# Attention softmax denominators out of the weighing product, and a new order of TensorE's blocks in a one-core audio tower

## What is computed

```
h = silu([x, 1] W_h + b_h) W_o + b_o + [x, 1] W_r + b_r        # patches of 16 samples, hidden 512
a = layernorm(h); q, k, v = a per head times Wq, Wk, Wv         # 16 heads of 16, 64 tokens per batch row
h = h + softmax(q k / sqrt(256)) v W_out + b_out
h = h + real(ifft(fft(layernorm(h)) w)) + bias
```

## Time and profile before

| | |
|---|---|
| median of 3 runs | 142.65 us (142.65 to 142.79) |
| the profiled execution: its own time | 142.76 us |
| the profiled execution: its span | 141.0 us |
| mean granted clock of TensorE | 0.993 of full |
| busy, share of the span | PE 94%, PEld 80%, DVE 79%, POOL 67%, ACT 61% |
| DMA packets | 24508 |

### The profile page before, as it was taken

The page is one execution under the profiler, slowest core; times in us unless marked ns, Lnnn a source line. Parts: engine busy times, 40 slices in busy tenths (PEclk is TensorE's granted clock), DMA queues, the critical chain, the costliest instruction groups (busy, mean ns, idle before and its releaser), DMA issues.

```text
span 141.0 us, 6132 instructions
## 1 busy us (share of the span) xinstructions
PE 132.8 (94%) x2444; PEld 112.4 (80%) x2444; DVE 111.6 (79%) x337; ACT 85.7 (61%) x245; POOL 94.7 (67%) x186
## 2 busy tenths in 40 slices
PE   6879999999999998999999999999999999999861
PEld 2469999999997876978878889889788788788540
DVE  5584596859978578798898898988988988978751
ACT  4374765477878584865947747649558477455110
POOL 3284796996583364677687686786876876773361
PEclk9999999999999999999999999999999999999997
DMA  4678000030000010121312302203113123031102
GB/s 70 157 174 257 14 0 0 0 36 11 2 0 5 5 19 5 19 50 15 63 37 23 60 12 49 56 7 65 46 15 60 37 23 59 6 60 41 38 0 74
DMA packets 24508, 5.89 MB, mean 42 GB/s; under 512 B 20384, under 2 KB 24224, under 8 KB 24480
## 3 DMA queue, kind: packets, MB, share of 16 engines
q1 hardware_dynamic: 24192, 5.37, 18.3%
q10 hardware_dynamic: 288, 0.13, 0.3%
HBM read 2.35 MB, written 2.10 MB: 32 GB/s over the span
## 4 chain that ended last, share of the span: by engine, by line
PE 78%; DVE 7%; POOL 4%; issue 3%; DMA 3%; ACT 1%; SPq 1%; POOLq 0%; DVEq 0%
PE bank L1036 11%; PE bank L954 11%; PE bank L1022 7%; PE bank L1099 6%; PE bank L1075 5%; PE bank L959 5%; PE bank L1080 4%; PE bank L1120 4%; PE bank L1064 3%; DMA wf_raw<-in_W_r 3%; PE bank L1049 2%; PE bank L1133 2%; PE bank L948 2%; PE bank L1103 2%; PE bank L1124 2%
## 5 line engine op out<-in xcount | busy, mean ns | idle before, releaser
L824 DVE TENSOR_REDUCE bank<-bank 128x4 f32<-128x256 f32 x64 | 22.8, 425 | 6.9 <-ACT pT L376 6.5
L376 ACT ACTIVATE pT<-bank 128x256 f32<-128x256 f32 x64 | 19.4, 391 | 2.5 <-PE bank L1049 2.5
L1036 PE MATMUL bank<-qT,xzT 32*128 32x64 f32 x512 | 17.9, 276 | 0.0
L1036 PEld LDWEIGHTS bank<-qT,xzT 32*128 32x128 f32 x512 | 15.7, 186 | 2.7 <-issue 2.7
L695 DVE TENSOR_TENSOR hid_lo<-bank,hid_hi 128x512 fp32r<-128x512 f32 x16 | 11.0, 685 | 7.5 <-ACT bank L344 7.5
L582 POOL TENSOR_TENSOR side_lo<-sideT,side_hi 128x256 fp32r<-128x256 f32 x14 | 10.2, 728 | 8.3 <-ACT sideT L386 8.3
L545 POOL TENSOR_SCALAR xblk<-xh,parity_sb 128x128 f32<-128x128 f32 x32 | 11.5, 372 | 5.9 <-PE bank L1080 4.8
L371 ACT ACTIVATE maxT<-bank 128x128 fp32r<-128x128 f32 x16 | 4.4, 277 | 17.8 <-PE bank L1058 17.8
L593 POOL TENSOR_TENSOR on_lo<-onT,on_hi 128x256 fp32r<-128x256 f32 x14 | 10.3, 737 | 7.1 <-ACT on_hi L390 6.8
L553 POOL TENSOR_TENSOR hb_all<-h_all,bout_bc 128x256 f32<-128x256 f32 x16 | 11.5, 735 | 4.0 <-ACT h_all L348 4.0
L361 ACT ACTIVATE xzT<-bank,parity_sb 128x256 f32<-128x256 f32 x28 | 12.0, 498 | 0.0
(11 more groups left out here) (166 smaller groups left out, 386.8 us busy)
## 6 DMA issues: line engine op xcount, KB each, us to landing
out<-y SPq DMA_DIRECT2D x16, 128.0 KB, 1.7
xblk<-xh SPq DMA_DIRECT2D x32, 32.0 KB, 2.5
wo_raw<-in_W_o SPq DMA_DIRECT2D x1, 512.0 KB, 4.2
wout_raw<-in_W_out SPq DMA_DIRECT2D x1, 256.0 KB, 2.9
fr<-in_wr SPq DMA_DIRECT2D x1, 256.0 KB, 4.3
fi<-in_wi SPq DMA_DIRECT2D x1, 256.0 KB, 4.3
minus_raw<-in_minus_rows SPq DMA_DIRECT2D x1, 128.0 KB, 2.2
bout_bc<-in_b_out SPq DMA_DIRECT2D x1, 128.0 KB, 3.5
```

Source lines behind the costliest of these rows:

```text
L376: nc.scalar.activation(pT[:, j, :], bank[j][:, D:2 * D], ACT.Exp).then_inc(exp_done, 1)
L824: nc.vector.tensor_reduce(rowmax[:, j, :], bank[j][:, 0:D].rearrange("p (h k) -> p h k", k=TOK), AX_X, ALU.max).then_inc(max_done, 1)
L1036: pe.matmul(bank[j][:, at0:at0 + TOK], xzT[t % 3][rows32, 2 * half + b, :, :].rearrange("p e k -> p (e k)"), qT[t % 3][rows32, half, TOK * ...
```

## The change

The denominators come out of the same products that weigh x. xblk is now, for each of two batch rows and 16 heads, 32 columns wide: 16 of x and 16 of ones, which a memset sets once. A product covers the 64 rows of one head's keys instead of the 128 of two, so there are 32 of them; the even heads' results go to one PSUM bank, the odd heads' to another, and in both 16 rows are weighed x and 16 the denominator. VectorE transposes both banks at once (128x512) and takes reciprocals of one column per block; GpSimd multiplies (VectorE in the last two tiles); VectorE transposes the quotients into onT. Nothing crosses heads any more, so there are no zeros to keep, and all placing is done by four DMAs per tile. TensorE's project moves to the front of the following step, mix_freq takes tile i-2 instead of i-1, turn_side behind query. The queues of the other engines follow. xh, h2b and rstd2 have three buffers, the row maxima move into the score banks, and x, the sides and the maxima change banks.

```
+    on_rows, weighedT, xh[3], h2b[3], rstd2[3];  xblk: [P, 2, D] -> [P, 2, 2*QUADS, 2*HD], memset to 1.0
-    pair_ones (constant, load and tile), sumsT, inv_rows
@@ sync
-            def place_crossed(t):      # two DMAs
+            def place(t):
                 sp.wait_ge(xh_set, t + 1)
                 if t >= 2:
                     sp.wait_ge(pv_done, t - 1)
+                heads = xh[t % 3][:].rearrange("p (g e d) -> p g e d", e=2, d=HD)
                 for b in range(2):
+                    for e in range(2):
+                        sp.dma_start(xblk[t % 2][TOK * e:TOK * e + TOK, b, :, 0:HD],
+                                     heads[TOK * b:TOK * b + TOK, :, e, :]).then_inc(xblk_placed[t % 2], 16)
+            for i in range(T + 3):
                 if i + 2 < T:
-                    place_crossed(i + 2)
-                if i >= 1:
-                    store(i - 1)
+                    place(i + 2)
+                if i >= 3:
+                    store(i - 3)
@@ scalar, step(i) after:
+    copy_xT(i+3), copy_max(i+1), copy_xzT(i+3), exponent(i+1), lead_on(i), copy_q(i+3), copy_side(i-1)
+    copy_q(t) waits for side_turned t-3 (from t = 4)
@@ gpsimd
-            def place_same(t): ...
+            def divide(t):
+                pool.wait_ge(inv_done, t + 1)
+                nc.gpsimd.tensor_tensor(on_rows[:].rearrange("p c e d -> p e c d"), weighedT[:, :, :, 0:HD],
+                                        inv_sum[:].unsqueeze(3).to_broadcast([P, 2, D // 32, HD]),
+                                        ALU.mult).then_inc(on_divided, 1)
+    step(i): divide(i), split_side(i-2), add_bias(i-1), normalize(i+4), inv_std2(i-1), split_on(i)
@@ vector
+            def invert(t):
+                dve.wait_ge(pv_done, t + 1)
+                if t >= 1:
+                    dve.wait_ge(on_divided, t)
+                nc.vector.transpose(weighedT[:].rearrange("p e c r -> p e (c r)"), weighed[:, :, 0:D]).then_inc(pv_turned, 1)
+                dve.wait_ge(pv_turned, t + 1)
+                nc.vector.reciprocal(inv_sum[:], weighedT[:, :, :, HD]).then_inc(inv_done, 1)
+            def turn_on(t):
+                dve.wait_ge(on_divided, t + 1)
...
+                nc.vector.transpose(onT[:].rearrange("p a t -> p (a t)"),
+                                    on_rows[:].rearrange("p c e d -> p (c e d)")).then_inc(on_set, 1)
+    step(i): invert(i), [divide(i) from tile 14], residual(i-1), finish(i-3), turn_on(i), variance2(i-1),
+             split_x(i+3), maximum(i+2) x4, split_max(i+2)
+    after the loop: finish(13), residual(15), finish(14), variance2(15), finish(15)
@@ tensor
             def scores(t):
+                if t >= 1:
+                    pe.wait_ge(max_lo_set, t)
             def turn_max(t):
+                    pe.wait_ge(pv_turned, t)
             def weigh(t):
-                for j in range(QUADS):
-                    pe.matmul(bank[PV_BANK][32 * j:32 * j + 32, D:2 * D], pair_ones[:], pT[:, j, :], start=True, stop=True)
...
+                        for e in range(2):
+                            for j in range(QUADS):
+                                last = pe.matmul(bank[PV_BANK[e]][32 * j:32 * j + 32, cols],
+                                                 xblk[t % 2][TOK * e:TOK * e + TOK, b, QUADS * half + j, :],
+                                                 pT[TOK * e:TOK * e + TOK, j, cols], start=True, stop=True)
             def mix_freq(t):
+                if t < T - 2:
+                    pe.wait_ge(h2_done, t + 2)
             def project(t):
+                    pe.wait_ge(h2_done, t)
+                if t >= 3:
+                    pe.wait_ge(y_set, t - 2)
             def turn_x(t):
+                if t >= 3:
+                    pe.wait_ge(pv_turned, t - 2)
             def step(i):
+    project(i-1), scores(i+2), turn_x(i+3), turn_max(i+1), keyed_scores(i+1), take_max(i+1),
+    mix_freq(i-2), query(i+3), turn_side(i-1), [in step 15: mix_freq(14), project(15)], weigh(i+1)
+    after the loop: turn_side(15), mix_freq(15)
```

More of the change, by code:

```diff
@@ L156, in audio_tower_kernel @@
         h2 = [sb(f"h2_{i}", [P, D]) for i in range(2)]
-        h2b = [sb(f"h2b{i}", [P, D]) for i in range(2)]
+        h2b = [sb(f"h2b{i}", [P, D]) for i in range(3)]
         stats2 = sb("stats2", [P, 6])
@@ L160, in audio_tower_kernel @@
         ve2 = sb("ve2", [P, 1])
-        rstd2 = [sb(f"rstd2_{i}", [P, 1]) for i in range(2)]
+        rstd2 = [sb(f"rstd2_{i}", [P, 1]) for i in range(3)]
         y = [sb(f"y{i}", [P, D]) for i in range(2)]
-        bank = [ctx.enter_context(nc.psum_tensor(f"bank{i}", [P, 512], F32)) for i in range(8)]
+        score_banks = ctx.enter_context(nc.psum_tensor("score_banks", [P, QUADS, 512], F32))
+        bank = [score_banks[:, j, :] for j in range(QUADS)]
+        bank.append(ctx.enter_context(nc.psum_tensor("bank4", [P, 512], F32)))
+        weighed = ctx.enter_context(nc.psum_tensor("weighed", [P, 2, 512], F32))
+        bank += [weighed[:, 0, :], weighed[:, 1, :], ctx.enter_context(nc.psum_tensor("bank7", [P, 512], F32))]
         bank16 = [b[:].bitcast(BF16) for b in bank]
@@ L878, in step @@
             def step(i):
-                if i < T:
+                invert(i)
+                if i >= WHOLE_ON:
                     divide(i)
+                if i >= 1:
+                    residual(i - 1)
+                if i >= 3:
+                    finish(i - 3)
+                turn_on(i)
                 if i >= 1:
@@ L888, in step @@
                     split_max(i + 2)
[L889 to L894 removed]
+            dve.wait_ge(blocks_set, 3)
             for j in range(QUADS):
@@ L906, in _ @@
             mean_shift(3)
-            for i in range(T + 1):
+            for i in range(T):
                 step(i)
+            finish(T - 3)
+            residual(T - 1)
+            finish(T - 2)
+            variance2(T - 1)
+            finish(T - 1)
         @block.tensor
@@ L1063, in turn_side @@
                 for half in range(HALF):
-                    last = pe.transpose(bank[SIDE_BANK][:, D + half * P:D + (half + 1) * P],
+                    last = pe.transpose(bank[SIDE_BANK][:, half * P:(half + 1) * P],
                                         h2[t % 2][:, half * P:(half + 1) * P], ident[:])
@@ L1078, in weigh @@
                         cols = slice(half * P + TOK * b, half * P + TOK * (b + 1))
-                        for j in range(QUADS):
-                            last = pe.matmul(bank[PV_BANK][32 * j:32 * j + 32, cols],
-                                             xblk[t % 2][:, b, half * P + 32 * j:half * P + 32 * j + 32],
-                                             pT[:, j, cols], start=True, stop=True)
+                        for e in range(2):
[3 more added lines that the diff above has]
+                                                 pT[TOK * e:TOK * e + TOK, j, cols], start=True, stop=True)
                 last.then_inc(pv_done, 1)
@@ L1166, in step @@
             def step(i):
+                if i >= 1:
+                    project(i - 1)
                 if 0 <= i + 2 < T:
                     scores_inputs(i + 2)
+                    scores(i + 2)
+                if 3 <= i + 3 < T:
+                    turn_x(i + 3)
+                if 0 <= i + 1 < T:
+                    turn_max(i + 1)
+                    keyed_scores(i + 1)
+                    take_max(i + 1)
+                if i >= 2:
+                    mix_freq(i - 2)
+                if 0 <= i + 3 < T:
+                    query(i + 3)
                 if i >= 1:
                     turn_side(i - 1)
-                if 0 <= i + 1 < T:
-                    turn_max(i + 1)
-                if 3 <= i + 3 < T:
-                    turn_x(i + 3)
-                if 0 <= i + 2 < T:
-                    scores(i + 2)
-                if 0 <= i + 1 < T:
-                    keyed_scores(i + 1)
-                    take_max(i + 1)
-                if i >= 1:
+                if i == T - 1:
                     mix_freq(i - 1)
-                if 0 <= i < T:
                     project(i)
-                if 0 <= i + 3 < T:
-                    query(i + 3)
                 if i == -1:
@@ L1228, in _ @@
             cols_spectrum(0)
-            for i in range(-1, T + 1):
+            for i in range(-1, T):
                 step(i)
+            turn_side(T - 1)
+            mix_freq(T - 1)
 _INS = {
```

185 lines of the change are left out of this document (78 added, 107 removed).

## The result

| | before | after |
|---|---|---|
| median | 142.65 us (142.28 to 142.79, 4 runs) | 145.52 us (145.15 to 146.67, 4 runs) |
| profiled: own time, span | 142.76, 141.0 us | 145.84, 144.0 us |

After over before is 1.0207, 95% interval 1.0155 to 1.0259: clearly slower, by about 2%. The forecast was 141.0 us (139.0 to 143.8), faster. So it was wrong, in sign and in range.

What follows compares the result with a forecast made beforehand. TensorE, busy 94% of the span, sets the 5.56 us step. Gains of 2.5 (12 steps x 0.21), 0.6 (first steps) and 0.44 (steps 13, 14) less 1.9 (tail) give 1.65: 141.0 us, range 139.0 to 143.8.

Steps and rivals of the forecast that it cites:

- wrong at the root: The prediction's sign of its own basic failure: TensorE's step above 5.5 us with TensorE never idle.
- The weighing, 0.62: TensorE's weighing: 64 half-height records, eight at once, 0.43 us plus the scores' overhead of 0.20, where 0.56 were seen.
- the bound of 0.0175 per record (1.12): Upper bound for the weighing: 64 records starting no faster than in the old weighing, 1.12 us.
- TensorE's new order: TensorE's reordered middle step: blocks with entry 0.11 and exit 0.09 per shape change sum to 5.35 us, 0.21 less.
- The last steps: Steps 13 and 14: both end on the exponents, at 5.0 and 4.35, 9.35 us together instead of 9.79.
- The tail: From the last weighing to the last y: 8.6 us instead of 6.7, so 1.9 lost.
- mix_freq(13) to 2.9: In the tail: mix_freq of tile 13 follows the residual at 1.9 and is done 2.9 us after the last weighing.
- First steps: Start of the kernel: step 0 ends at 54.97 instead of 55.57 us, 0.6 gained, good to some 0.3.
- VectorE: VectorE's work per step falls from 4.97 to 4.82 us, under 5.35, with its first transpose growing to 0.71.
- GpSimd: GpSimd per step: two placing passes of 0.372 go, one division of 0.74 comes, 4.24 us of work.
- rival C: GpSimd's ring closes: on_lo comes too late for project, steps of 5.55 to 5.6, 143.4 us; chance 15%.
- Rival D: Half-height products pack no closer than full-height ones: weighing 1.12, half a microsecond more per step, 148.5 us; chance 10%.

Runs made afterwards that it cites:

- e1: Changed kernel with the weighing in 16 products of 128 columns instead of 32 of 64, half of the weighed values wrong: 142.15 us, 0.9952 of the kernel before.
- e13: Kernel before plus one 128-column identity transpose a step between scores and keyed scores, adding a change of shape: 145.84 us, ratio 1.0215.
- e15: Kernel before plus one rounded 128-column product a step between scores and keyed scores, adding changes of shape and kind: 145.80 us, ratio 1.0210.
- e5: Changed kernel with 24 weighing products, first 8 of 128 columns, then 16 of 64, some outputs wrong: 145.28 us, 1.0156 of the kernel before.
- e2: Changed kernel with all 32 weighing products streaming 128 columns instead of 64, half of the weighed values wrong: 149.47 us, 1.0467 of the kernel before.
- e12: Kernel before plus one 128-column identity transpose a step behind turn_x, adding no change of shape or kind: 144.34 us, ratio 1.0100.
- e14: Kernel before plus one 128-column identity transpose a step between mix_freq and project, adding a change of kind: 144.01 us, ratio 1.0091.
- e16: Kernel before plus one rounded 128-column product a step between mix_freq and project, adding no change of shape or kind: 144.11 us, ratio 1.0094.
- e7: Changed kernel with TensorE's step regrouped to two full-shape blocks between tiled ones instead of three: 149.77 us, 1.0492 of the kernel before.

## Why the prediction was wrong

The forecast of the span was 1.65 us less; it became 3.0 more, 4.65 off: 3.25 in the twelve steps, 0.78 in steps 13 and 14, 0.76 in the tail, less 0.14 that the first steps gained beyond the forecast. The prediction's own sign of being "wrong at the root", a step above 5.5 with TensorE never idle, is what came. By its own terms:

- **The weighing, 0.62.** This term failed: 0.79. It came from the scores, which start eight records at a time. The first half of the new weighing does exactly that, so "eight at once" was right. But the scores are 16 products and the new weighing is 32, and behind the sixteenth comes a gap and a slower pace. Nothing of before shows 32 small products in a row of one kind with so few columns; the bound of 0.0175 per record (1.12) was the only trace of such a limit in the forecast. It is 12 x 0.17 = 2.0 of the miss in the twelve steps, and 0.34 in the next two. With 16 products the step came out as forecast (e1), and with it the time only 1.15 over the forecast, the rest of the miss being in the last two steps and the tail.
- **TensorE's new order.** Right in every block to 0.01; a change of shape was shown to cost something by itself (e13, e15). The sum was 5.35, and e1 measured 5.34. The twelve steps took 67.45 for the forecast's 64.2: of these 3.25 the weighing is 2.0 and the stalls 0.94.
- **Stalls of issue** (0.94) were not foreseen, and are not explained.
- **The last steps.** Steps 13 and 14 took 10.13 for 9.35: the weighing twice (0.34), and a wait of turn_max for the dearer transpose of weighedT (0.32), which the forecast had priced for VectorE but not followed to who waits for it; step 14 has no scores to cover it. The remaining 0.12 is small differences.
- **The tail**, 9.36 from the end of the last weighing to the last y for 8.6. The first step of the sum that failed is "mix_freq(13) to 2.9": it ended at 3.2, because it doesn't go on behind the residual (1.9) but waits for y(12), which comes behind that residual on VectorE. The forecast had y(13) as mix_freq(14)'s wait and missed the same wait one tile earlier. From the end of y(13) to the residual of tile 15 the two plain blocks, with a wait for sideT, took 2.25 where the forecast had 1.95, and the way from turn_side to y(15) 2.66 for 2.5. The bulk of the loss, 1.9, was foreseen.
- **First steps** 0.6, measured 0.74. **VectorE** 4.82 a step, measured 4.82, transpose 0.72 for 0.71; **GpSimd**'s division 0.62 for 0.74, its work 4.03 a step for 4.24 (4.22 by the forecast's own terms); **ScalarE**'s exponents held TensorE by 0.15 and 0.16 in steps 13 and 14, and not in the twelve. No wait for on_lo: rival C did not happen. Rival D had the right place and the wrong price: "half-height products don't pack" was said to cost 0.5 a step; they do pack, what costs is their number, and it costs 0.17.
- The Trainium skill's rule (TensorE: Matmul & The Clock Gate, section "Wait — 56ns, not 53.3ns?"), no two matmuls closer than about 25 ns, would have made 64 records 1.6 us. They took 0.79, so the rule doesn't hold across tiles of the array: even behind the sixteenth product a record begins every 11 ns.

By the count: 0.46 a step saved with the denominators, 0.23 lost in the weighing (0.79 for 0.56), 0.21 in one more full-shape block (project 0.20, the transposes 0.09, query -0.08), and the rest in differences of 0.01. That is nothing gained, in twelve steps, for a tail that is 2.66 longer.

## What to carry to other kernels

Count the small products of a block as well as their columns: sixteen fp32 products of 64 columns here began at the array's pace, and the further ones came slower. Merging two kinds of work into one product can give back much of the gain if it doubles the number of products (0.23 of 0.46 here), and a block moved alone between tiled work costs its change of shape (0.20 here). When a stage moves behind the next tile's, follow its wait chain through the last two tiles by hand, every shared bank included, since nothing overlaps it there.

## What the runs showed of the hardware

- fp32 products of 64 or 128 columns on eight 64x32 tiles, in the changed kernel and in e5: sixteen begin at eight records per 56 or 109 ns, then a gap of some 0.08 us, then the others at 11 (32 narrow products) to 13 ns a record (e5). With 128 columns in all of them (e2) there is no gap, and the last 32 records begin in 0.48 us.
- A full-shape instruction alone between tiled products takes 0.26 us, transpose or rounded product alike; inside full-shape work it adds 0.13.
- Between plain fp32 transposes and rounded products there is no price (5.69 us a step in e12, e14 and e16).
- In e7 two waits, for x_lo and for weighedT, end while TensorE's pipeline drains and are not listed as its idle time in the twelve steps, though the first product of query behind one of them takes 0.23 us for 0.12.
